# Aggregation and experts of a graph network as one program, with expert shares applied on chip and scatter-adds into the output

## What is computed

```python
x = x + att(ln(x), adj)                 # softmax(leaky(s1 + s2), masked by adj) @ (h @ fc_w + fc_b)
x = x + capacity_ffn(ln(x))             # router to 64, top 2, capacity 256, gelu(h @ w1.T + b1) @ w2.T + b2
# mean aggregation
h = ln(x); deg = adj.sum(1) + 1e-5
x = x + relu((adj / deg) @ h @ W_neigh.T + b_neigh + h @ W_self.T + b_self)
# experts: 8 experts, the 2 best of each row
h = ln(x); logits = h @ Wg + bg
v, idx = top_k(logits, 2); w = softmax(v)
a, g = split(h @ W1[e] + b1[e]);  y_e = (silu(a) * g) @ W2[e] + b2[e]
x = x + sum over the two e of w_e * y_e
```

## Time and profile before

| what | value |
|---|---|
| median of three runs | 1240.36 us (1239.25 to 1242.32) |
| the profiled execution's own time | 1240.98 us |
| its span from first to last instruction | 1239.2 us |
| PE busy | 1042.0 us, 84% of the span |
| DVE, ACT, POOL busy | 832.6, 618.6, 210.9 us |
| moved by DMA | 168.92 MB |

### The profile page before, as it was taken

How to read it: one execution, slowest core, us unless ns; L and a number is a source line. 1 busy time by engine, 2 the same in 40 slices (tenths; PEclk the granted TensorE clock), 3 DMA queues, 4 the chain that set the end, 5 groups by cost and what they waited for, 6 DMA issues and landing times. The chain is left out here.

```text
span 1239.2 us, 23376 instructions
## 1 busy us (share of the span) xinstructions
PE 1042.0 (84%) x7664; PEld 829.2 (67%) x7665; DVE 832.6 (67%) x1827; ACT 618.6 (50%) x725; POOL 210.9 (17%) x226
## 2 busy tenths in 40 slices
PE   4768999999999699789986999991299999999930
PEld 3448888888889589578744888880166666666620
DVE  7469999999995556876662566752355556555626
ACT  2659999999993576458731121210133333333300
POOL 1000000000000000017781045433011121111210
PEclk9899999999999699899997999995699999999975
DMA  9937777777720312112107999951811111111127
GB/s 285 283 123 220 230 227 218 235 215 248 212 69 2 106 69 69 68 69 87 51 1 175 201 197 242 227 117 56 334 48 55 51 51 55 51 55 51 51 90 257
DMA packets 71978, 168.92 MB, mean 136 GB/s; under 512 B 7697, under 2 KB 57744, under 8 KB 65392
## 3 DMA queue, kind: packets, MB, share of 16 engines
q1 hardware_dynamic: 47120, 92.99, 24.1%
q0 software_dynamic: 12464, 40.14, 14.7%
q10 hardware_dynamic: 12336, 35.00, 7.9%
HBM read 144.92 MB, written 45.35 MB: 154 GB/s over the span
## 5 line engine op out<-in xcount | busy, mean ns | idle before, releaser
L586 PE MATMUL PS<-G,PT 128*128 128x256 f16 x2028 | 229.6, 273 | 0.0
L586 PEld LDWEIGHTS PS<-G,PT 128*128 128x128 f16 x2028 | 198.4, 98 | 22.4
L1450 PE MATMUL sum<-H,adjTh 128*128 128x257 f16 x676 | 154.7, 276 | 11.6 <-DMA adjTh<-adjT_dram 11.6
L1452 PE MATMUL sum<-H,adjTh 128*128 128x256 f16 x676 | 154.7, 276 | 0.0
L1823 DVE SCALAR_TENSOR_TENSOR hb<-ePsH,w_unscale,eb 128x1024 f32<-128x1024 f32 x59 | 75.7, 1284 | 89.8 <-PE ePsH L1744 89.8
L1744 PE MATMUL ePsH<-W,xT_hi 128*128 x472 | 122.7, 383 | 4.7 <-DVE xT_lo L1814 4.7
L1780 ACT ACTIVATE xT_hi<-ePsX 128x256 f16<-128x256 f32 x59 | 22.6, 384 | 180.4 <-PE ePsX L1733 180.4
L1764 PE MATMUL ePsY<-W,actT 128*128 x472 | 111.6, 380 | 0.2 <-issue 0.2
L573 PE MATMUL PS<-ident,probs 128*128 128x128 f32 x676 | 89.7, 280 | 22.8 <-DVE PT L434 21.1
L434 DVE SCALAR_TENSOR_TENSOR PT<-PS,PT 128x1024 f16<-128x1024 f32 x104 | 103.4, 1015 | 4.4 <-ACT PT L283 4.4
L1719 POOL DMA_INDIRECT results_dram<-ys,place x59 | 56.8, 962 | 277.5 <-DVE ys L1840 273.0
(11 more groups left out here) (284 smaller groups left out, 1822.2 us busy)
## 6 DMA issues: line engine op xcount, KB each, us to landing
adjf<-adj_dram SPq DMA_DIRECT2D x26, 1664.0 KB, 8.1
slot_rows<-blank SPq DMA_DIRECT2D x26, 1028.0 KB
adjTh<-adjT_dram POOLq DMA_DIRECT2D x26, 832.0 KB, 9.5
W<-eW_dram ACTq DMA_DIRECT2D x12, 1024.0 KB, 4.9
d_stage<-eW_dram ACTq DMA_DIRECT2D x8, 1024.0 KB, 7.5
xs<-slot_rows SPq DMA_DIRECT2D x59, 128.5 KB, 2.1
results<-results_dram ACTq DMA_DIRECT2D x12, 512.0 KB, 10.4
eb<-eb_dram SPq DMA_DIRECT2D x1, 4096.0 KB, 13.8
```

What stands on the lines that cost most here:

```text
L586: mm = nc.tensor.matmul(acc[u][:, 0:D], left, right, start=(j == 0 and n == 0), stop=(j == T - 1 and n == 2))
L1450: nc.tensor.matmul(acc[u][:, 0:D + 1], left, H[:, j, 0:D + 1], start=(j == 0), stop=False, skip_group_check=True)
L1452: mm = nc.tensor.matmul(acc[u][:, 0:D], left, H[:, j, D + 2:2 * D + 2], start=False, stop=(j == T - 1), skip_group_check=True)
```

## The change

1. Stages 3, 4 and 5 become one program, `aggregation_and_experts`, with no barrier between. Its parts of on-chip memory are carved from rooms that are done with: the experts' biases lie in the room of `own` and `H`, W2 in that of the weight stage and the adjacency buffers, the loop's tiles in X. SP stores X to the output pair by pair during the aggregation. ACT and SP load weights and biases at the end of the aggregation. The experts' tables have somewhat fewer steps.
2. The shares are applied in the expert loop. A slot row gets one word more (ROW = D + 2): the difference of the two logits. ACT computes tanh of its half, DVE makes the share of it, ACT scales the product (`yw`) and the second bias (`bw`) with it, and POOL adds the two into `ys`. The place is now the row number, the same for both experts of a row.
3. POOL's scatter goes to the output itself and adds (`compute_op=ALU.add`). `results`, the fetch, the combination and the last store are gone.
4. POOL issues the first four adjacency tiles in the feed-forward, at slot 52, into the room of the feed-forward's first operand, once all hidden parts are done. The aggregation's loads begin with tile 4.
5. In the feed-forward `normalise_row` moves from POOL to DVE, and turning and projecting come one slot earlier. `expert_peak` on DVE is replaced by `expert_square` on ACT for the first weights; the squares of the second weights and of the first biases go.
6. The experts' first weights are split in the order 4, 5, 6, 7, 0, 1, 2, 3.

The core of the diff:

```diff
@@ capacity_ffn
-        ROWS_AT, NORMAL_AT, TURN_AT, PROJECT_AT = 32, 38, 42, 44
+        ROWS_AT, NORMAL_AT, TURN_AT, PROJECT_AT = 32, 38, 41, 43
@@ POOL
-            for slot in range(ROWS_AT, SLOTS):
-                for i in row_at(slot, NORMAL_AT):
-                    normalise_row(i)
+            for slot in range(ROWS_AT, ROWS_AT + T):
+                if slot == 4 * NCH:
+                    pool.wait_ge(hidden, 4 * NCH)
+                    for i in range(NADJ):
+                        pool.dma_start(t["adj_early"][i], dram["adjT"][i, :, :]).then_inc(t["adj_in"][i], 16)
                 for i in row_at(slot, ROWS_AT):
                     residual(i)
@@ ACT
-                if 3 <= c < 3 + E1:
+                if 2 <= c < 2 + E1:
+                    expert_square(c - 2)
+                if 3 <= c < 1 + E1:
                     expert_load(c - 1)
@@ DVE
-            def invert_deviation(i):
+            def normalise_row(i):
...
+                wait(dve, rows_turned, r - 1)
+                v.tensor_scalar(h[:, r % 2, s, :], X[:, i, :], moments[:, i, 0:1], row_rstd[:, i:i + 1], ALU.subtract,
+                                ALU.mult).then_inc(rows_done, 1)
...
-                if 2 <= c < 2 + E1:
-                    expert_peak(c - 2)
@@ aggregation_and_experts, SP
+            for i in range(0, T, 2):
+                sp.wait_ge(x_ready, i + 2)
+                sp.dma_start(rows_out[:, i:i + 2, :], X[:, i:i + 2, :]).then_inc(x_stored, 16)
+                if i >= 20:
+                    for e in range(i - 20, i - 18):
+                        sp.dma_start(b1[:, e, :], dram["eb1"][:, e, :]).then_inc(b1_in, 16)
...
+            for q in range(NROW):
+                sp.wait_ge(scattered[q], 64 * ((T // 2 + NROW - 1 - q) // NROW))
+            sp.wait_ge(tables_ready, 1)
...
@@ ACT
+                if due(s):
...
+                    nc.scalar.activation(balance[:, ds(s, 1)], kept[:, ds(s, 1), 1], ACT.Tanh,
+                                         scale=0.5).then_inc(balanced, 1)
+                if due(s - 3):
...
+                    nc.scalar.activation(bw[1 - u][:, :], b2[:, e, :], ACT.Copy,
+                                         scale=weight[:, ds(s - 3, 1)]).then_inc(bw_ready, 1)
...
+                    nc.scalar.activation(yw[1 - u][:, :], psY[1 - u][:, 0:D], ACT.Copy,
+                                         scale=weight[:, ds(s - 3, 1)]).then_inc(yw_ready, 1)
...
+            nc.scalar.activation(junk[:, :], eps[:, :], ACT.Silu).then_inc(table_set, 1)
@@ DVE
+                dve.wait_ge(token_ready, i // 2 + 1)
+                for k in range(2):
+                    v.tensor_tensor(rows[:, row_slot(i), :, k, D + 1], best[:, k, i:i + 2], best[:, 1 - k, i:i + 2],
+                                    ALU.subtract).then_inc(gap_ready, 1)
...
+                if due(s - 3):
+                    dve.wait_ge(balanced, s - 2)
+                    v.tensor_scalar(weight[:, ds(s - 3, 1)], balance[:, ds(s - 3, 1)], 0.5, 0.5, ALU.mult,
+                                    ALU.add).then_inc(weighed, 1)
...
@@ POOL
             def load(i):
                 if live(i):
-                    wait(pool, acc_ready, i - NADJ + 1)
+                    wait(pool, acc_ready, i - NADJ + 1 if i >= 2 * NADJ else 0)
                     pool.dma_start(adjh[i % NADJ][:, :], adjv[i, :, :]).then_inc(adj_in[i % NADJ], 16)
...
-            for i in range(NADJ - 1):
+            for i in range(NADJ, 2 * NADJ - 1):
                 load(i)
             for i in range(0, TOTAL, 2):
-                load(i + NADJ - 1)
-                load(i + NADJ)
+                load(i + 2 * NADJ - 1)
+                load(i + 2 * NADJ)
                 if live(i - 6):
                     scatter(i - 6)
...
             def store(s, u):
+                settled(pool, store_waits, (bw_ready, s + 1), (yw_ready, s + 1))
+                nc.gpsimd.tensor_tensor(ys[u][:, :], yw[u][:, :], bw[u][:, :], ALU.add).then_inc(ys_ready, 1)
                 settled(pool, store_waits, (ys_ready, s + 1), (place_ready, s + 1))
                 if not isinstance(s, int) or s > 0:
 
                     settled(pool, store_waits, (stored[1 - u], 8 * (s + u)))
-                pool.indirect_dma_start(out=dram["results"], in_=ys[u][:, :], in_offset=None,
-                                        out_offset=bass.IndirectOffsetOnAxis(ap=place[u][:, 0:1], axis=0)
-                                        ).then_inc(stored[u], 16)
+                pool.indirect_dma_start(out=out, in_=ys[u][:, :], in_offset=None,
+                                        out_offset=bass.IndirectOffsetOnAxis(ap=place_i[u][:, 0:1], axis=0),
+                                        compute_op=ALU.add).then_inc(stored[u], 16)
```

More of the change, by code:

```diff
@@ L31 @@
 assert T % 2 == 0 and NP - N < P
+ROW = D + 2
 def wait(eng, sem, value):
@@ L641 @@
 E1 = 8
+NADJ, NROW, TURN_ROWS_AT = 4, 4, 8
 F1 = 512
@@ L1336, in _, with aggregation_and_experts @@
                     expert_scales()
-NADJ, NROW, TURN_AT = 4, 4, 8
-def mean_aggregation(nc, t, dram):
+def aggregation_and_experts(nc, t, dram, out):
     with ExitStack() as ctx:
@@ new lines, in aggregation_and_experts @@
+        yw, bw, ys = ([carve(D) for _ in range(2)] for _ in range(3))
+        over = carve(E1 * T).rearrange("p (e t) -> p e t", e=E1)
+        passed = carve(NS * E1).rearrange("p (s e) -> p s e", s=NS)
+        free += E1 * D + 4 * F1
+        moved = tables[:, free:free + NS * E1].rearrange("p (s e) -> p s e", s=NS)
+        reached = carve(E1 * E1).rearrange("p (a b) -> p a b", a=E1)
+        expert, source = sb("expert", [P, NS], I32), sb("source", [P, NS], I32)
+        limits, tile_no, low = sb("limits", [P, E1, T]), sb("tile_no", [P, NS, E1]), sb("low", [P, E1, E1])
@@ L1372, in mean_aggregation @@
+        psY = [PS[:, 6 + u, :] for u in range(2)]
+        adj_in = t["adj_in"]
         ones_set = sem("d_ones")
@@ L1385, in mean_aggregation, with due, tile_expert, last_tile_over @@
         TOTAL = T + 6
+        src = dram["slot_rows"].rearrange("(s p) d -> s p d", p=P)
+        E_FIRST, E_LAST, E_TOTAL = 6, NS - 3 + (NS - 1) % 2, NS + 4
+        SPLIT_ORDER = [4, 5, 6, 7, 0, 1, 2, 3]
+        def due(s):
+            return not isinstance(s, int) or 0 <= s < NS
+        def tile_expert(eng, s):
+            return eng.value_load(expert[0:1, ds(s, 1)], min_val=0, max_val=E1 - 1)
+        def last_tile_over(first, last):
+            slots = range(first * 2 // NP, -(-last * 2 // NP))
+            return max(max(i for i in range(T) if ADJ_PLACE[i % NADJ] == q) for q in slots)
         def live(i):
@@ L1501, in _, with turn_slots @@
                     count(i - 4)
+            last = chosen[(T // 2 - 1) % 2]
+            pe.wait_ge(logits_taken, T // 2)
+            for n, right in enumerate((running[:, :], last[:, 0, :], last[:, 1, :])):
+                mm = nc.tensor.matmul(psR[:, 0:E1], ones[:, :], right, start=(n == 0), stop=(n == 2))
+            mm.then_inc(total_ready, 1)
+            def turn_slots(s, u):
+                pe.wait_ge(x_in[u], 8 * (s - u) + 16)
+                wait(pe, lo_ready, s)
+                for k in range(KD):
+                    mm = nc.tensor.transpose(psX[:, k * P:(k + 1) * P], xs[u][:, k * P:(k + 1) * P], ident[:, :])
+                mm.then_inc(x_turned, 1)
@@ new lines, in _ @@
+            step(v.tensor_reduce(ends[:, :], reached[:, :, :], AX_X, ALU.add))
+            v.tensor_scalar(move[:, :], tiles[:, :], -1.0, float(T), ALU.mult, ALU.add).then_inc(table_chain, 1)
+            step.count += 1
+            step(v.tensor_tensor(passed[:, :, :], tile_no[:, :, :],
+                                 ends[:, :].unsqueeze(1).to_broadcast([P, NS, E1]), ALU.is_ge))
+            v.tensor_reduce(expert_f[:, :], passed[:, :, :], AX_X, ALU.add).then_inc(table_chain, 1)
+            step.count += 1
```

618 lines of the change are left out of this document (252 added, 366 removed).

## The result

The changed kernel takes 1268.15 us (median of 4 runs, 1266.6 to 1268.99), the kernel before 1239.8 beside it: a ratio of 1.0228 (95% interval 1.0209 to 1.0246), 2.3% slower. The forecast was 1224, with a range to 1266. The profiled execution has a span of 1266.4 us against 1239.2, so 27.2 are to be found. The table cuts both spans at the same marks of the timeline (before: the earlier trace rows, and of each pair of products the first is taken, whence 834.8).

What follows compares the result with a forecast made beforehand. PE was taken to bound the expert loop and fill the aggregation, with idle seams around. Feed-forward -11, first seam -11.8, aggregation +64, second seam -21.5, end -36: -16.3; 1240.98 - 16.3 - 0.6 = 1224, own range 1205 to 1240, overall 1198 to 1266.

Steps and rivals of the forecast that it cites:

- Aggregation: Aggregation stage: PE's work unchanged, but a new wait for normalised rows costs +64 us, bounds 55 and 98.
- scatter j behind tile j+10, ring of four, stall, clock at half: Aggregation: pair j's scatter waits for tile j+10, four-row ring stalls PE 8.0 us, half-speed restart costs 2.5; six times.
- For j = 12 ... 1 to 2 us: Aggregation, pair 12: its second load waits for tile 21 only, so PE stalls just 1 to 2 us.
- Expert loop: Expert loop: PE's work per tile unchanged at 4.99 us, added work and scatter hidden beside it, 0 us change.
- X: Expert loop: surplus of the adding scatter's pitch over the plain 3.2 us, taken as 1.0, giving pitch 4.2.
- a rival that costs 59 x (pitch - 4.99): Expert loop: accumulating scatter sets the pace through POOL's landing wait; at pitch 6.0, +60, 1284 us; chance 0.26.
- The end: Behind the expert loop: last landing at 1198.2, plus 5.1 between landing and next program, 1203.3; -36 us, bounds -33, -39.
- Feed-forward: Feed-forward: peaks leaving DVE, normalise leaving POOL, and one slot less save 11 us: 5.5 in chunks, 5.5 in the tail.
- If DVE became the pace, the lower bound holds: Feed-forward's last stretch: DVE's slack hides the moved normalise; gain 5.5 us, bounds 1 and 8, 1 if DVE paces.
- First seam: Between feed-forward and aggregation: early tiles save 8.8 us, no clock fall with a 2.9 us gap saves 3.0; -11.8.
- (a): Rival, aggregation: no stall, scatters are released earlier than read from the queue; 64 less, 1160 us; chance 0.10.
- (c): Rival, expert loop: ACT changes tables in each tile, tanh behind Silu; +24, 1248 us; chance 0.04.

Runs made afterwards that it cites:

- undoing POOL's order: Kernel after, but in each aggregation step POOL requests tiles i+3 and i+4, then scatters pair i-6, instead of i+7 and i+8 first: 1190.7 us.
- plain scatters: Kernel after with `compute_op=ALU.add` left out of the experts' scatter, so it writes without adding: 1252.52 us.
- the late tiles: Kernel after, but the first four adjacency tiles are requested by the aggregation's program, not in the feed-forward: 1278.61 us.
- four-buffer run: Kernel after with four buffers of places in place of two, so DVE waits for the scatter four tiles back: 1253.73 us.
- the run with POOL's order and the place written later: Kernel after with POOL's aggregation order undone and DVE writing the place behind its product, two buffers kept: 1175.85 us.

## Why the prediction was wrong

**Aggregation: right in mechanism, mis-sized.** The steps (scatter j behind tile j+10, ring of four, stall, clock at half) all stand in the trace, the number of long stalls too, and undoing POOL's order gave the time back. Several sizes were off. The long stalls were 9.4 us on average where I took 8.0 (8.4 us in all). The landing that counts is that of the last of four scatters; the median of 6.0 is over all scatters, and in each of these groups the first takes longest (6.5 to 7.3). The chain that ended last has these six, from issue to landing:

```profile
728.91 4.56 DMA slot_rows<-rows,slot_i
753.29 4.53 DMA slot_rows<-rows,slot_i
777.42 6.62 DMA slot_rows<-rows,slot_i
804.16 4.82 DMA slot_rows<-rows,slot_i
828.61 4.51 DMA slot_rows<-rows,slot_i
852.64 6.19 DMA slot_rows<-rows,slot_i
```

The profile counts a landing from the start of the issue. I had added my 3.4 behind its end, which is 4.4 on the profile's count: close for four of the six, and 2 us short for the two longest stalls (10.79 and 10.38). The rest is about 0.5 us at the start, where POOL's tile load begins some 0.3 us behind the end of the tile, for which I had put nothing. "For j = 12 ... 1 to 2 us" was 4.4 and a restart of 3.1, 7.5 together. The other six restarts cost 2.6 on average, not 2.5. And the 3.0 that I took off for the clock behind the first seam came to 1.3.

**Expert loop: the failed step.** I wrote "All lie beside PE. At risk is the scatter: each waits until the one before has landed", and took X = 1.0, hidden, with a rival that costs 59 x (pitch - 4.99) through POOL's wait. X as I used it, the surplus of the scatters' pitch, is 1.4 to 2.1 (4.6 to 5.3 us from issue to issue, against 3.2), up to twice what I took. Even so POOL's wait would have been harmless, as three runs show. What I missed in the diff is that DVE's wait for the buffer of places had moved from behind its product to the head of the iteration, ahead of hb, and that the loop then runs at landing and hop, 5.18 us, in place of PE's 4.97. I had counted DVE's instructions and not asked what is queued behind its waits. By the rival's formula the measured 5.18 gives +11; so its size was reached, by another wait.

**The end.** Forecast 22.3 us behind the last hb, measured 30.2: 18.7 to the last scatter's issue (1254.88), 3.8 to its landing, 7.7 to the end. To the landing it is 22.5 where I had 17.2. Adding makes 4.0 of it (26.2 in all with plain scatters), and I had 3; most of the rest is what I had put at 0.3, for the results go out further back: the last plain scatter is issued 14.5 us behind the last hb (1237.3 - 1222.8), before 10.7. For the 7.7 I had used the 5.1 between two programs of the kernel before: the wrong row for a last program. It was also counted from 1194.9, where the profile has that scatter land 2.4 us behind its issue, at 1194.1.

**Feed-forward.** "If DVE became the pace, the lower bound holds": DVE did become it, and the bound did not hold. The chunks gave about what was forecast (G_lo and earlier together 6.5 us less waiting, 5.5 forecast), the tail gave some of it back. Over ten profiles the gain is 3.5 us, not 11; my bound of 1 for the tail was too good.

**First seam.** The fetch was priced right (8.8, and 8.6 by the late tiles). The clock was not. I expected no fall with a gap of 2.9 us. The gap was 2.75 in the kernel after, and the clock fell (0.57 from 654 to 658), 1.4 us behind the restart.

**The rivals.** (a) and (c) are out: the stall is there, and the expert loop has no table load. The one load that answers to the change stands ahead of it:

```profile
L1521 ACT ACT_TABLE_LOAD  x1: 1283/1283/1283, 909.6 to 909.6; - x1
```

Tanh takes 0.19 us behind each Silu. The sets that the Trainium skill lists (ScalarE: Activation LUTs, "Table sets") name none with Silu; as far as they go, they don't tell this case, and the trace decides. Of the adding scatter, the rule of the Trainium skill that I weighed (Collectives: The Full Stack, "The bandwidth ceiling": two source reads, twice the traffic, measured there on large transfers) would give 0.4 us. The runs show 1.4 to 2.0 in the landing, of which 0.6 is the longer issue, so traffic alone is not the price here.

The order of my chances was wrong too. I gave 0.71 to faster because a gain of 16 us was left between +64 and -80; errors of a tenth in such terms, all to one side, take nearly all of it, and my 1205 to 1240 allowed only 16 for them.

## What to carry to other kernels

When a diff changes how far ahead a queue asks for something, look at what stands behind that request in the same queue, and let a request that waits for the future never stand ahead of work that is due: one order of three lines was worth 77.5 us here. A wait has a place as well as a price: the same landing cost 12 to 14 us in front of hb and nothing behind the product. And where gains and losses of 60 to 80 us nearly cancel, each landing in them must be taken from the rows most like it in what is in flight, and added from where the profile counts it (the start of the issue), and the range must be as wide as their errors.

## What the runs showed of the chip

- A scatter of 128 rows of 1 KB by indices with addition holds POOL 1.56 us and lands 3.8 us after its issue; plain 0.96 (0.99) and 2.4. With a fetch of 129 KB issued 1.25 us behind it, it lands at 4.3 to 4.5. In the four-buffer run fetches at 1.24 to 1.26 gave 4.3 to 4.5 (8 scatters) and those at 0.5 to 0.9 gave 3.8 to 4.1 (10); plain scatters landed at 2.4 or 2.5 at every phase seen (1.2 to 1.6). In the kernel after, with two buffers, 18 of 20 fetches from 1059 to 1159 came at 1.24 to 1.26, and their scatters landed at 4.3 to 4.5. That the waits of the two loops hold each other in this phase is a reading; no run shows it.
- The same gap of 2.75 us of PE at the first seam was followed by a fall of the clock in some executions and not in others. The kernel after had 0.57 from 654 to 658 and needed 25.0 us for the first four tiles; the run with POOL's order and the place written later, with the same feed-forward and the same gap, had this row, and needed 23.4:

```profile
653.00:658.00 5.00, 5.00 (x45) 4.38 (x46) 0.00 (x0) 0.00 (x0) 2.20 (x4) 1.00 0.87 281
```

- The feed-forward ended at 647.9 to 652.6 us in ten profiles of what is nearly the same code up to there; the three latest, 650.6 to 652.6, are those in which the clock was granted at 0.91 to 0.95 from 600 to 620. A term of 2 us can't be read from a single pair.
